# One 128 by 260 edge product per sub-block in a graph attention layer: ScalarE copies each head's piece out of PSUM

## The reference, cut to what matters

```python
h = jnp.einsum('nd,hdf->nhf', x, W)                  # 6250 nodes, 4 heads of 64 features
e = leaky_relu(a_src[src] + a_dst[dst], 0.2)         # one logit per edge and head
ex = jnp.exp(e - emax[dst])
denom = segment_sum(ex, dst)                         # sums over a node's incoming edges
out = segment_sum(h[src] * (ex / denom[dst])[:, :, None], dst)
```

## Time and profile before

| | us |
|---|---|
| time, median of 3 runs | 2542.84 |
| fastest and slowest of the 3 | 2538.41, 2550.55 |
| profiled execution: span from first to last instruction | 2898.3 |

### The profile page before, as it was taken

How to read it: one execution, slowest core, us unless ns; L and a number is a source line. 1 busy time by engine, 2 the same in 40 slices (tenths; PEclk the granted TensorE clock), 3 DMA queues, 4 the chain that set the end, 5 groups by cost and what they waited for, 6 DMA issues and landing times. The chain is left out here.

```text
span 2898.3 us, 56530 instructions
## 1 busy us (share of the span) xinstructions
PE 1655.7 (57%) x17359; PEld 1267.0 (44%) x17359; DVE 1538.2 (53%) x5813; ACT 687.3 (24%) x2082; POOL 1778.3 (61%) x1803
## 2 busy tenths in 40 slices
PE   6566664556566334443443366765666666557894
PEld 5334433434444223332332344554554454346783
DVE  5544445556666444544544555565564655453443
ACT  4222221112221112122122123224322233323220
POOL 1666666666666666666666665656566666645774
PEclk9666565655555555555555566777777667668997
DMA  9356555534454453365365467667656765547987
GB/s 297 109 163 166 163 159 152 174 96 124 122 155 116 118 127 104 96 181 149 107 175 152 135 179 220 177 187 210 195 161 198 219 205 147 158 125 218 250 235 207
DMA packets 317811, 480.53 MB, mean 166 GB/s; under 512 B 77671, under 2 KB 241593, under 8 KB 312893
## 3 DMA queue, kind: packets, MB, share of 16 engines
q0 software_dynamic: 90960, 237.28, 31.2%
q1 hardware_dynamic: 217420, 231.05, 25.9%
q10 hardware_dynamic: 9120, 8.49, 0.9%
HBM read 399.71 MB, written 110.47 MB: 176 GB/s over the span
## 5 line engine op out<-in xcount | busy, mean ns | idle before, releaser
L1264 POOL DMA_INDIRECT region<-node_table,src_idx x1612 | 1573.9, 976 | 926.4 <-remote 489.0
L1454 PE MATMUL ps_p<-region 128*32 128x65 f32 x12896 | 405.9, 293 | 779.6 <-DVE region L1702 614.0
L1454 PEld LDWEIGHTS ps_p<-region 128*32 128x32 f32 x12896 | 311.6, 153 | 884.6 <-DVE region L1702 690.5
L1710 DVE SCALAR_TENSOR_TENSOR acc<-ps_p,region,acc 128x65 f32 x806 | 192.9, 280 | 805.1 <-remote 750.4
L1330 ACT ACTIVATE ps_p<-region 128x16 f32<-128x16 f32 x403 | 75.5, 187 | 1033.7 <-DVE region L1696 553.3
L1326 ACT ACTIVATE region<-ps_s 128x128 f32<-128x128 f32 x403 | 111.3, 276 | 835.3 <-PE ps_s L1436 384.5
L1436 PE MATMUL ps_s<-ident,region 128*128 128x128 f32 x403 | 170.2, 422 | 215.2 <-DVE region L1696 120.7
L1702 DVE TENSOR_TENSOR region<-region,ps_p 128x512 f32<-128x512 f32 x403 | 273.3, 678 | 24.0 <-ACT ps_p L1330 11.9
L1440 PEld LDWEIGHTS ps_s<-region 128*128 128x128 f32 x806 | 215.5, 294 | 75.4 <-issue 49.9
L1436 PEld LDWEIGHTS ps_s<-ident,region 128*128 128x128 f32 x403 | 105.6, 262 | 238.2 <-DVE region L1696 132.8
L1440 PE MATMUL ps_s<-region 128*128 128x32 f32 x806 | 191.0, 327 | 6.7 <-issue 6.6
(11 more groups left out here) (371 smaller groups left out, 2663.0 us busy)
## 6 DMA issues: line engine op xcount, KB each, us to landing
region<-in_W_dram SPq DMA_DIRECT2D x84, 512.0 KB
expert_in<-run_rows SPq DMA_DIRECT2D x280, 130.0 KB
region<-node_table,src_idx POOLq DMA_INDIRECT x1612
acc<-in_W_dram SPq DMA_DIRECT2D x28, 512.0 KB
region<-expert_in SPq DMA_DIRECT2D x47, 260.0 KB
acc<-base_rows SPq DMA_DIRECT2D x13, 896.0 KB
qkv_rows<-region SPq DMA_DIRECT2D x49, 194.0 KB
y_rows<-acc SPq DMA_DIRECT2D x28, 256.0 KB
```

Of the source, the lines that this page charges most:

```text
L1264: pool.indirect_dma_start(out=rows[:, s, j, :], out_offset=None, in_=table[:, :], in_offset=bass.IndirectOffsetOnAxis(ap=src_idx[:, n * SU ...
L1454: m = pe.matmul(ps_p[s % 2][h * WIN:(h + 1) * WIN, 0:HC], wts[:, s % 2, j, h, :], rows[:, s, j, h * HC:(h + 1) * HC], start=j == 0, stop=j ...
L1710: m = dve.scalar_tensor_tensor(out=a, in0=ps_p[s % 2][:, 0:HC], scalar=here[:, k, at(n)], in1=a, op0=ALU.mult, op1=ALU.add)
```

## The change

One `matmul` per sub-block takes all 128 weight columns (4 heads by 32 nodes) against the whole 260 numbers of a row. The result is 128 by 260: each head's rows now also hold products with the other heads' features, which nothing reads. Four copies on ACT take from each head's 32 partitions its own 65 columns into a new buffer `head_sums` in SBUF (two of them, by block), and raise `heads_ready`. The product of block n waits for `heads_ready` of n - 2 where it waited for `block_done`; POOL still waits for `block_ps`. The exponentials move to columns 260 to 275 of the bank.

DVE's `prepare` is split in two, and its order becomes `logits(n)`, `prepare_logits(n + 3)`, `weigh(n)`, `accumulate(n - 1)`, `prepare_masks(n + 3)`. `accumulate` waits for `heads_ready` and reads `head_sums`. On ACT the copies of block n - 1 stand between the exponential of n and the mask copy of n + 2.

```diff
             def ex_ps(s):
-            return ps_p[s % 2][:, P:P + SUB * G_HEADS].rearrange("p (j h) -> p j h", h=G_HEADS)
+            return ps_p[s % 2][:, SUMS_W:SUMS_W + SUB * G_HEADS].rearrange("p (j h) -> p j h", h=G_HEADS)
...
+            def own_heads(n, s):
+
+                act.wait_ge(block_ps, n + 1)
+                if n >= 2:
+                    act.wait_ge(block_done, n - 1)
+                for h in range(G_HEADS):
+                    r = slice(h * WIN, (h + 1) * WIN)
+                    m = act.activation(head_sums[r, s % 2, :], ps_p[s % 2][r, h * HC:(h + 1) * HC], ACT.Copy)
+                m.then_inc(heads_ready, 1)
+
             def body(n, s, ahead=2):
                 act.wait_ge(logits_ready, n + 1)
                 act.activation(ex_ps(s), lg[:, s % 2], ACT.Exp).then_inc(ex_ready, 1)
+                if n >= 1:
+                    own_heads(n - 1, s + SL - 1)
...
-                if not isinstance(n, int) or n >= 2:
-                    pe.wait_ge(block_done, n - 1)
+                if n >= 2:
+                    pe.wait_ge(heads_ready, n - 1)
                 for j in range(SUB):
-                    for h in range(G_HEADS):
-                        m = pe.matmul(ps_p[s % 2][h * WIN:(h + 1) * WIN, 0:HC], wts[:, s % 2, j, h, :],
-                                      rows[:, s, j, h * HC:(h + 1) * HC], start=j == 0, stop=j == SUB - 1)
+                    m = pe.matmul(ps_p[s % 2][:, 0:SUMS_W], wts[:, s % 2, j].rearrange("p h w -> p (h w)"),
+                                  rows[:, s, j, 0:SUMS_W], start=j == 0, stop=j == SUB - 1)
                 m.then_inc(block_ps, 1)
...
-                dve.wait_ge(block_ps, n + 1)
+                dve.wait_ge(heads_ready, n + 1)
                 dve.wait_ge(block_done, n)
...
-                    m = dve.scalar_tensor_tensor(out=a, in0=ps_p[s % 2][:, 0:HC], scalar=here[:, k, at(n)], in1=a,
+                    m = dve.scalar_tensor_tensor(out=a, in0=head_sums[:, s % 2, :], scalar=here[:, k, at(n)], in1=a,
...
             def body(n, s, ahead=3):
+                more = ahead == 3 or n + 3 < BLOCKS
                 logits(n, s)
-                if not isinstance(n, int) or n >= 1:
+                if more:
+                    prepare_logits(n + 3)
+                weigh(n, s)
+                if n >= 1:
                     accumulate(n - 1, (s + SL - 1) % SL)
-                weigh(n, s)
-                if ahead == 3 or n + 3 < BLOCKS:
-                    prepare(n + 3, s + 3)
+                if more:
+                    prepare_masks(n + 3)
```

More of the change, by code:

```diff
@@ L831, in main_stage @@
     XT, XN = 3, 3
+    SUMS_W = G_HEADS * HC
     A0 = 4
@@ L1016, in main_stage @@
         q_sum = sb("q_sum", [P, XG * M_HEADS])
+        head_sums = sb("head_sums", [P, 2, HC])
         x_in = [sem(f"x_in{i}") for i in range(X_GROUPS)]
@@ L1023, in main_stage @@
         self_done = sem("self_done")
+        heads_ready = sem("heads_ready")
         h_ps, h_ready, w_mean = sem("h_ps"), sem("h_ready"), sem("w_mean")
@@ L1398, in _ @@
                     carried.scalar(act, m, 4)
+            own_heads(BLOCKS - 1, (BLOCKS - 1) % SL)
         @block.tensor
@@ L1678, in _, with prepare_logits, prepare_masks @@
                 dve.wait_ge(table_out[i], 16 * XG * ((X_GROUPS + 1 - i) // 2))
-            def prepare(n, s):
+            def prepare_logits(n):
                 c = dve.value_load(column[0:1, at(n)], min_val=0, max_val=ACC_C - 2)
                 own.do(dve.tensor_scalar(t8[:, 0, :], drep[:, bass.ds(c, 1), :].squeeze(1), here[:, 0, at(n)], None, ALU.mult))
-                own.do(dve.scalar_tensor_tensor(out=t8[:, 1, :], in0=drep[:, bass.ds(c + 1, 1), :].squeeze(1),
-                                                scalar=here[:, 1, at(n)], in1=t8[:, 0, :], op0=ALU.mult, op1=ALU.add))
+                own.step(dve.scalar_tensor_tensor(out=t8[:, 1, :], in0=drep[:, bass.ds(c + 1, 1), :].squeeze(1),
+                                                  scalar=here[:, 1, at(n)], in1=t8[:, 0, :], op0=ALU.mult, op1=ALU.add))
+            def prepare_masks(n):
+                own.wait()
                 own.step(dve.tensor_tensor(dsel[:, n % ML], bm, bcast(t8[:, 1, :], 1, SUB), ALU.mult))
@@ L1716, in body @@
             def body(n, s, ahead=3):
+                more = ahead == 3 or n + 3 < BLOCKS
                 logits(n, s)
-                if not isinstance(n, int) or n >= 1:
+                if more:
+                    prepare_logits(n + 3)
+                weigh(n, s)
+                if n >= 1:
                     accumulate(n - 1, (s + SL - 1) % SL)
-                weigh(n, s)
-                if ahead == 3 or n + 3 < BLOCKS:
-                    prepare(n + 3, s + 3)
+                if more:
+                    prepare_masks(n + 3)
             for n in range(3):
-                prepare(n, n)
+                prepare_logits(n)
+                prepare_masks(n)
             dve.wait_ge(mix_loads, 16 * MIX_LOADS)
```

## The result

| | median us | lowest to highest | runs | ratio to before, 95% interval |
|---|---|---|---|---|
| before | 2543.85 | 2538.41 to 2550.55 | 4 | |
| after | 2579.77 | 2577.88 to 2589.64 | 4 | 1.0148 [1.0124, 1.0173] |
| after, repeated later (chip 13) | 2587.92 | 2586.74 to 2589.81 | 4 | 1.0168 [1.0146, 1.0191] |

The profiled execution of after took 2589.64 us, its span is 2587.6 us, the mean clock of TensorE 0.863. The span stands 2 us under the time this time, not 355 us above it.

What follows compares the result with a forecast made beforehand. The prediction took POOL's pace to bound unrecorded runs: 81 (start) + 2088 + 11 + 295 (tail) = 2475 us. Adding 35 of the remaining 68 us gave 2510 us, range 2430 to 2610.

Steps and rivals of the forecast that it cites:

- The hold: TensorE's semaphore release after a block's product: 3.7 us of each traced round, at most 3.0 us in unrecorded runs.
- POOL's pace of 5.18 us: POOL's gathers and sends set 5.18 us a block; with start and tail the kernel takes 2475 us.
- decoupling weights from sums should help in about half: DVE's new order wins about half of the 68 us above POOL's pace; 35 us of them remain.
- So a longer product costs nothing there as long as PE as a whole stays under 5.18 us a block.: PE's product, 2.5 or 1.3 us longer, costs nothing while PE's total load stays under POOL's pace.
- The change touches neither the gathers nor the tail: Gathers on POOL and the 295 us tail after the blocks stay as in the trace.
- DVE has less: 4.3 us a block: DVE's work over the whole stage, without idle time before the adding, is 4.3 us a block, under POOL's 5.18.
- The 68 us: Median of before above POOL's 2475 us, 0.17 us a block: all the change can win.
- the link of 1.2 us: ACT's four copies between product and sum: 1.0 us, about 1.2 with wait and semaphore.
- The late rival: From 1600 us on PE bounds the blocks at 5.9 us each, 2610 us in all; chance 0.26.
- above 5.6 us a block: Sign of PE bounding the late stage: a period above 5.6 us a block from 1600 to 2600 us.
- Nothing to win: Rival: POOL paced the unrecorded runs, its own stalls and transfers make the 68 us; 2543 us, chance 0.22.
- The real hold: Rival: TensorE's release delay is real and goes by PE instruction count; fewer instructions give 2400 us, chance 0.12.

Runs made afterwards that it cites:

- before_again: The kernel before, unchanged and profiled a second time, without the long wait for TensorE's release: 2547.37 us, span 2545.3.
- with pairs: After with each sub-block's product made as two of 64 by 130 side by side, copies and new order kept: 2560.13 us, ratio 1.0059 to before.
- with heads: After with before's product of 32 matmuls of 32 by 65 per block, copies and new order kept: 2555.09 us, ratio 1.003 to before.
- after_again: The changed kernel, unchanged and run once more, the table's repeated line: 2587.92 us, ratio 1.0168 to before.

## Why the prediction was wrong

- **The hold "cannot be as long" in the runs compared: right, the reason wrong.** I took it for a matter of recording. It was in the execution that the trace came from, recorded or not, and not in those that were timed. To sum against a second bound was still sound.
- **POOL's pace of 5.18 us, floor 2475 us: right up to block 257** (5.13 us in before_again, 5.16 in after).
- **The failed step is the sum's term "decoupling weights from sums should help in about half", minus 33 us, with the product put at nothing: "So a longer product costs nothing there as long as PE as a whole stays under 5.18 us a block."** The new order alone returned nothing (0.9987), and the product cost 25 to 35 us. TensorE did stay under: it was busy 421 of 600 us in after's early stretch and 459 of 600 in the late one (rows below), 3.6 and 4.5 us a block. The average load says nothing about the rounds behind a burst, in which nobody waits for POOL. In the burst shown, the longer product makes VectorE wait for the copies and ScalarE for the transpose behind it. Over the late stretch the first of these waits grows from 5.6 to 26 to 30 us. That such rounds make up the whole cost is argued.
- **"The change touches neither the gathers nor the tail": the tail took 8 to 13 us longer.** The sum had kept it at 295. The cause is open.
- **"DVE has less: 4.3 us a block" hid the late bound.** It was a mean over the whole stage of a held trace. Late, VectorE has the expert tiles and routing steps beside its blocks, and about 0.6 us of register load in each, and the pace is 5.75 us a block, above POOL's. Moving that load took the pace to 5.48 and gave 40 us. The 68 us to be won were there, and not in the order of weights and sums.
- **The copies: the link of 1.2 us was right** (1.1 us from the product's end at 1653.57 to the adding at 1654.66), and its price was not given by itself. It was about 9 us.
- **The product's length: 3.6 and 1.9 us said, 3.83 and 1.92 measured.**
- **The late rival (0.26, 2610 us)** had the place and the sign, not the mechanism. It named 5.9 us a block, and 5.90 were measured, but 5.75 of them were in the kernel before, so that number was luck. So was the sign "above 5.6 us a block", which before meets too. Its own test, a mean clock below 0.80, was not met (0.88).
- **"Nothing to win" (0.22)** was right about the order, wrong about the 68 us, of which moving a register load returned 40, and lacked the price of product and copies.
- **The real hold (0.12).** The unrecorded 5.35 us come out only at the upper of its two figures for an instruction, 66 ns (64 x 0.066 + 1.1 = 5.3); the lower one gives 5.07. The runs compared had no hold to remove.
- The measured time lies 70 us above the forecast, inside the range of 2430 to 2610. It is there by the room left for a late bound that did not come about as described.

The stretches of after for the third and the eighth point, columns as in the earlier trace rows:

```profile
1000.00:1600.00 600.00, 420.94 (x1658) 339.14 (x1659) 360.41 (x1442) 251.07 (x991) 442.66 (x452) 0.81 0.65 186
1600.00:2200.00 600.00, 459.13 (x1988) 382.18 (x1987) 379.41 (x1469) 277.61 (x952) 404.60 (x414) 0.88 0.68 203
```

## What to carry to other kernels

A pace set by one engine hides what others do only while every burst fits into the lead of the buffers. Cost an edit by the rounds behind a burst, where the engines catch up, and read the load of each stage apart. Before a trace is taken as the kernel's, compare its span with the times: here they differed by 14% in the one that misled and by 2 us in those that did not. Look for "issue" in front of an instruction that follows a register load; moved behind a long instruction it cost hardly anything here and gave 40 us.

## What the runs showed of the hardware

- The same program takes 2546 us on four chips and 2905 to 2911 us on two. In the slow traces the semaphore of a block's 32 products rises a median 3.65 us behind their last recorded end, in the others 0.04 us. With no gather left it is soon there in a slow trace too.
- A column number loaded into a register costs VectorE 0.62 to 0.69 us of standing still ahead of the next instruction (L1697 in after, L1710 in before_again), and hardly anything behind one of 0.68 us (20.5 us over 403 blocks for L1728 in after).
- Two products of 64 weight columns side by side take 2.00 us a block where one of 128 takes 3.83 and four of 32 take 1.09, at the half clock. Halving the tile about halves the time at each step.
- A busier TensorE gets more clock: over the whole span 0.679 in before_again, 0.737 with pairs, 0.863 in after. From 1000 to 1600 us it was busy 334 of 600 us at 0.57 in before_again and 421 at 0.81 in after. That can give back part of a longer product: in one burst the same eight instructions of L773 take 3.62 us with heads and 1.89 in after_again.
